# Layer 0's input loaded in a turned layout, and its ternary weights made later, in a two-layer transformer kernel on one core

## What is computed

```python
x = _layernorm(x + _L0_attn_ref(x, w_qkv, w_out, b_out))
    # qkv = x @ w_qkv; 16 heads of 16; causal softmax(q k^T / 4) v; @ w_out + b_out
x = _layernorm(x + _L0_ffn_ref(x, W_up, W_gate, W_down))
    # scale = mean(|W|) + 1e-8; W -> clip(round(W / scale), -1, 1) * scale
    # (silu(x @ wu.T) * (x @ wg.T)) @ wd.T
x = _layernorm(x + _L1_attn_ref(x, ...))      # windowed, global and with linear biases
x = _layernorm(x + _L1_ffn_ref(x, ...))
```

## Time and profile before

| | |
|---|---|
| median of 3 runs | 1007.37 us (1007.07 to 1007.87) |
| time of the profiled execution | 1006.18 us |
| its span | 1004.5 us, 18031 instructions |
| PE busy | 950.5 us (95%) |
| PE weight loads | 516.3 us (51%) |
| DVE busy | 690.4 us (69%) |
| ACT busy | 593.1 us (59%) |
| POOL busy | 354.1 us (35%) |

### The profile page before, as it was taken

The page is one execution under the profiler, slowest core; times in us unless marked ns, Lnnn a source line. Parts: engine busy times, 40 slices in busy tenths (PEclk is TensorE's granted clock), DMA queues, the critical chain, the costliest instruction groups (busy, mean ns, idle before and its releaser), DMA issues. The chain is left out here.

```text
span 1004.5 us, 18031 instructions
## 1 busy us (share of the span) xinstructions
PE 950.5 (95%) x6546; PEld 516.3 (51%) x6546; DVE 690.4 (69%) x1529; ACT 593.1 (59%) x1210; POOL 354.1 (35%) x424
## 2 busy tenths in 40 slices
PE   6798999999998999988899999999999998999997
PEld 4453333333344887664334344343434354798896
DVE  2778888888843687578888888888888632433423
ACT  3434777777766345436577777777777767222321
POOL 3022123321222455234446354352615333323432
PEclk9798999999999999999799999999999999999999
DMA  7644111222000200152705142130401000000001
GB/s 245 198 157 123 48 39 43 65 64 64 2 2 15 81 1 8 45 176 55 221 2 177 29 150 84 53 118 19 136 1 40 2 1 1 1 1 22 22 1 42
DMA packets 32996, 64.20 MB, mean 64 GB/s; under 512 B 6095, under 2 KB 22367, under 8 KB 30532
## 3 DMA queue, kind: packets, MB, share of 16 engines
q1 hardware_dynamic: 31564, 58.47, 18.9%
q0 software_dynamic: 1072, 3.80, 1.1%
q10 hardware_dynamic: 272, 0.79, 0.2%
HBM read 50.45 MB, written 12.32 MB: 62 GB/s over the span
## 5 line engine op out<-in xcount | busy, mean ns | idle before, releaser
L1150 ACT ACTIVATE prob<-ps 128x512 f32<-128x512 f32 (+6 forms) x896 | 426.9, 541 | 158.9 <-PE ps L1195 155.9
L1195 PE MATMUL ps<-qop,kop 98*128 98x512 bf16 (+14 forms) x1376 | 271.4, 288 | 1.7 <-ACT prob L1150 0.6
L1181 PE MATMUL ps<-kop,qop 96*128 96x512 bf16 (+3 forms) x896 | 245.2, 359 | 14.8 <-DVE maxes L1080 11.2
L1195 PEld LDWEIGHTS ps<-qop,kop 107*128 107x128 bf16 (+1 forms) x1376 | 113.3, 97 | 212.8 <-ACT prob L1150 118.8
L1224 PE MATMUL ps<-prob,vst 128*32 128x512 f32 (+4 forms) x1792 | 211.2, 543 | 4.7 <-POOL prob L1017 2.9
L1080 DVE CUSTOM_DVE_ANT_0 sums<-ps,tri 128x128 bf16<-128x128 f32 (+7 forms) x256 | 180.6, 754 | 20.5 <-PE ps L1181 18.9
L1017 POOL TENSOR_TENSOR prob<-prob,keep 128x384 int32<-128x384 int32 (+2 forms) x144 | 121.7, 854 | 190.4 <-ACT prob L1150 189.9
L1080 DVE CUSTOM_DVE_ANT_0 sums<-ps,table 128x960 bf16<-128x960 f32 x128 | 148.0, 1156 | 48.2 <-PE ps L1181 35.9
L1625 PE MATMUL ps<-xs,wffn 128*128 128x512 f32 x640 | 156.1, 396 | 1.0 <-PEq L829 1.0
L1080 DVE CUSTOM_DVE_ANT_0 tri<-ps,table 128x960 bf16<-128x960 f32 x128 | 147.6, 1153 | 3.0 <-PE ps L1181 2.9
L1520 POOL TENSOR_TENSOR hs<-hf,hs 128x512 fp32r<-128x512 f32 x64 | 83.0, 1297 | 150.6 <-ACT hs L1543 142.3
(11 more groups left out here) (106 smaller groups left out, 693.0 us busy)
## 6 DMA issues: line engine op xcount, KB each, us to landing
table<-in_table SPq DMA_DIRECT2D x32, 464.0 KB, 4.5
qop<-q_parts SPq DMA_DIRECT2D x96, 128.0 KB, 2.6
kop<-k_parts SPq DMA_DIRECT2D x48, 128.0 KB, 2.6
kop<-k_parts SPq DMA_DIRECT2D x48, 96.0 KB
q_parts<-qop SPq DMA_DIRECT2D x8, 384.0 KB, 3.8
q_parts<-kop SPq DMA_DIRECT2D x8, 384.0 KB, 2.6
x<-in_x SPq DMA_DIRECT2D x4, 512.0 KB, 6.1
k_parts<-qop SPq DMA_DIRECT2D x4, 384.0 KB, 2.7
```

The lines of the kernel that those rows point to most:

```text
L1150: nc.scalar.activation(prob[0:rows, q % 2, k % HG, lo % CH:lo % CH + hi - lo], ps[0:rows, home["exp", n, k], lo % CH:lo % CH + hi - lo], A ...
L1181: last = nc.tensor.matmul(ps[:, S_BANK + score_slot(L, k)[0] + a // CH, a % CH:a % CH + b - a], qop[0:RD, par, h, i0:i0 + P], kop[0:RD, pa ...
L1195: return nc.tensor.matmul(ps[:, bank, a % CH:a % CH + b - a], lhs, rhs, start=start, stop=True, skip_group_check=True)
```

## The change

1. The host also hands over x transposed (`xt`, 256 x 2048). Four transfers of 512 KB bring it straight into `proj.xt`: the first two as SP's first work, the other two behind the constants. Layer 0 has no turns any more. `K.x` is loaded behind group 2's operands, in four transfers, for the residual steps of groups 1 to 4, and `ident` is first waited for by the transposition of group 0's output.
2. The opening's order: units 0 to 3 come first, then v and units 4 to 7, then v 2, 3 and 4; one v of batch 1 (the last) is put behind the last maximum. Four banks of PSUM take turns instead of three. The steps beside the maxima are spread by the maxima's columns plus 256. Load 1 of the operands comes behind the writes of units 8 to 11.
3. POOL asks for the weight matrices only once group 0's operands have landed. The abs steps lie behind units 10, 11 and 12; total and threshold behind group 0's rows.
4. The ternary step is cut in 12 slices of 128x512. POOL makes the lower comparison into a bf16 buffer `below` of its own, four slices in quads 4 to 7 of each of groups 0, 5 and 6. DVE makes the second comparison, three slices in each of the last four quads of group 6. The feed-forward waits for all 12 slices.

```diff
+BELOW_GROUPS, BELOW_QUADS = (0, N - 3, N - 2), (4, 5, 6, 7)
@@ plan_by_table
+        if group in BELOW_GROUPS and n in BELOW_QUADS:
+            steps.append(("below", 4 * BELOW_GROUPS.index(group) + BELOW_QUADS.index(n), 0))
+        if group == N - 2 and n >= nq - 4:
+            steps += [("ternary", 3 * (n - nq + 4) + k, 0) for k in range(3)]
@@ opening_of
-PE_SHARE = ({"turn": 1, "unit": 1, "v": 1}, {"turn": 0.85, "unit": 1.72, "v": 1.72})
+PE_SHARE = ({"turn": 0.6, "unit": 1, "v": 1}, {"turn": 0.85, "unit": 1.72, "v": 1.72})
...
+    width = [hi - lo if layer.index == 1 else hi - lo + 2 * P for _, _, lo, hi in units]
...
+    scale = [("total", 0, 0), ("threshold", 0, 0)] if layer.index == 0 else []
+    return out + [("parts", 0, 1), ("rows", 0, 1)] + scale + [("max", k, 2) for k in range(AHEAD[layer.index])]
@@ Projection
-        banks = ((4, 5, 6), (4, 5, 6)) if i == 0 else ((6, 7), (6, 7, 4, 5))
+        banks = ((4, 5, 6, 7), (4, 5, 6, 7)) if i == 0 else ((6, 7), (6, 7, 4, 5))
...
+        if self.i == 0 and b == 0:
+            return [u[0], u[1], f[0], u[2], f[1], u[3], f[2], f[3], v[0], u[4], u[5], f[4], v[1], u[6], f[5], u[7], f[6],
+                    v[2], f[7], v[3], ("v", TB // 2)]
         if self.i == 0:
...
+            return [u[0], u[1], f[0], u[2], f[1], ("abs", 0), u[3], f[2], ("abs", 1), v[1], u[4], f[3], ("abs", 2),
+                    u[5], f[4], v[2], u[6], f[5], u[7], f[6], f[7], v[3]]
@@ pool
+        elif what == "below":
+
+            j, cols, home = self.slice_of(k)
+            pool.wait_ge(self.tern, 3)
+            nc.gpsimd.tensor_scalar(self.below[:, home], self.raw[j][:, cols], self.thr[:, 1, j:j + 1], None, ALU.is_lt
+                                    ).then_inc(self.below_set, 1)
@@ dve
         elif what == "ternary":
-            dve.wait_ge(self.tern, 3 + 2 * k)
-            nc.vector.tensor_scalar(self.below, self.raw[k], self.thr[:, 1, k:k + 1], None, ALU.is_lt
-                                    ).then_inc(self.tern, 1)
...
+            j, cols, home = self.slice_of(k)
+            dve.wait_ge(self.tern, 3)
+            dve.wait_ge(self.below_set, k + 1)
+            nc.vector.scalar_tensor_tensor(out=K.wffn[:, j, 0, cols], in0=self.raw[j][:, cols],
+                                           scalar=self.thr[:, 0, j:j + 1], in1=self.below[:, home],
+                                           op0=ALU.is_gt, op1=ALU.subtract).then_inc(self.tern, 1)
@@ sync
+                for c in range(NC // 2):
+                    load_turned(c)
                 sp.dma_start(K.ident[:], dram.ident).then_inc(proj.ident_loaded, 16)
...
+                for c in range(NC // 2, NC):
+                    load_turned(c)
...
-            later = len(proj.units) // 2 + 2 * (1 - i)
+            later = len(proj.units) // 2 + 4 * (1 - i)
...
             operands.load(sp, BUFS - 1)
+            if i == 0:
+                for c in range(NC):
+                    sp.dma_start(K.x[:, CT * c:CT * c + CT, :],
...
@@ gpsimd
             pool.wait_ge(fills, FILLS)
+            if i == 0:
+                pool.wait_ge(loaded[0], 16 * operands.loads)
+                for j, wt in enumerate(dram.ffn[0]):
...
```

113 lines of the change are left out of this document (55 added, 58 removed).

## The result

| | before | change |
|---|---|---|
| median | 1007.62 us (1007.07 to 1008.41, 4 runs) | 1000.39 us (999.68 to 1003.08, 4 runs) |
| profiled execution, its span | 1006.18, 1004.5 us | 1003.08, 1001.3 us |

The ratio is 0.9933, 95% interval 0.9912 to 0.9953: faster, by 7 us instead of the 17 of the prediction, and outside its range of 983.0 to 995.5. Measured again beside other kernels it was 999.18 us (998.53 to 1003.58, 6 runs), ratio 0.9940 (0.9917 to 0.9964).

What follows compares the result with a forecast made beforehand. Up to 86 us a chain (x, units 0 to 3, write, load, 32 maxima, rows) sets the pace, then PE is full. First exponential gains 17.7 us; less 0.3 and 0.4, 17.0: 989.5 us, range 983.0 to 995.5.

Steps and rivals of the forecast that it cites:

- step 3: Opening: ACT's first sum waits for late weights, holding DVE and PE; 3.0 us plus 1.0 for PE's clock, bounds 0 to 8.
- step 2: Group 0's stretch of maxima, without four turns and one v: 30.5 us, between engines' own work and upper bound 33.1.
- step 1: Start: x lands at 6.9, no turns ahead, DVE's first maximum at 30.3 instead of 46.19; 15.9 us gained, bounds 12 to 17.
- Step 4: Total and threshold behind group 0's rows, partly on the path of group 1's maxima: cost 0.3 us, 0 to 0.8.
- Step 5: Ternary slices ahead of group 7's first gathering: 12 take 7.5 us, with POOL's comparisons mostly in idle time; cost 0.4, 0 to 3.
- two engines block each other: Rival near group 7's gathering: DVE slices and POOL's clearings hold each other up; 3 us more, 992.5; chance 0.10.
- Step 6: Loading K.x behind group 2's operands and load 1 behind unit 11's write: both in time, no cost.
- The rival of a slow comparison on POOL: POOL's ternary comparisons delay quad 8's clearing and PE in three groups; at 5.5 us each, 1019 us; chance 0.03.
- the first exponential (68.6): Sign that the opening's gain arrived: group 0's first exponential at 68.6 us against 86.32, a gain of 17.7.
- the stretch took over 39 us: Sign of being wrong: group 0's stretch of maxima takes over 39 us.
- more than 2 us of the gain at the first exponential: Sign of being wrong: over 2 us of the lead at group 0's first exponential are missing at the kernel's end.
- group 7's gathering at about 286: Mark for the gathering behind the ternary slices, which ran at 278.70 before: it would run at about 286 us.

Runs made afterwards that it cites:

- constants ahead: The change plus 22 unused matmuls of ones on PE while it waits for its first operands: 1001.37 us, ratio 0.9945.
- own matrices: The change, with each sum of magnitudes waiting only for its own weight matrix instead of all three: 994.55 us, measured again 995.69 us.
- the small clearings: The sums late, with GpSimd's causal clearing cut to 8 elements in group 7 (992.64 us), then groups 6 and 7 (992.21 us) of layer 0.
- the sums late: The change, with three sums of magnitudes moved behind unit 13's finish, v 6 and unit 14's finish: 992.79 us, measured again 995.80 us.

## Why the prediction was wrong

The direction and the places were right, the size was not: the forecast gain was 17.0 us, the median's is 7.2, and the profiled execution's 3.1. What failed are three terms of the sum, all ahead of the first exponential: step 3 (3.8 us too small), step 2 (3.2) and step 1 (2.4). The gain there was 7.8 us (78.51 against 86.32) and not 17.7. The largest, step 3, failed because the first sum of magnitudes waits for all three matrices, and not for the one it reads. Against the change's profile, by the steps:

**Step 1, the start: 15.9 us forecast, 13.5 measured.** "x is SP's first transfer, 0.45 us earlier, so it lands at about 6.9" took the landing of x for the start. The unit needs w too. Before, it landed at 5.7 (4.9 us after its request at 0.80), and PE was at its turns until 10.78; now it lands 7.3 us after its request, and PE waits until 8.10. Why it lands later stays open. It isn't the bytes asked for alone: with as many as before the change it took 7.1 us, and with 0.5 MB less 6.8. What the traces show beside it is that the queue of x had moved 1199 packets (1.13 MB) by 8 us before, and 596 packets (1.07 MB) in the change, so packets twice as large, beside the same 272 packets of w. No run tested it. And "two units take 3.85 us at first" was read behind 3.4 us of turns, that is from a PE already at work: the first units now come from rest, 1.9 us slower in sixteen records than with constants ahead. Before, PE came from rest at the turns, which took 3.4 us for sixteen records (eight take 1.09 us at full clock). The writes took 3.0 us to land against 2.6. From the loads' request to the first score it was 9.6 us, as said (9.8).

**Step 2, the stretch without the weights: 30.5 us forecast, 33.7 measured** (33.1 was my upper bound). Of the eleven profiles in which nothing waited for the weights six had 33.6 to 33.7 us and five 34.9 to 35.2. What parts them is one piece of PE's work at a lower clock: the v above, or the first unit of batch 1, which took 2.95 to 3.36 us in the other four, at a granted clock of 0.57 to 0.65, where it takes 1.94. In these four PE had waited 2.0 to 3.9 us for the keys before the first score. I chose near the sum of busy times. DVE had its 27 us of work, 27.13 of the 33.6 with own matrices, but waits for ACT's first parts six times, 6.1 us together: a unit passes PE, ACT and DVE in turn, and DVE, in order, stands until its turn comes. My error was to stay near the sum of busy times where three engines hand work to each other. That these waits are what lies between 30.5 and 33.7 is read from the trace; no run took them away.

**Step 3, the weights: 4.0 us forecast, 7.8 measured** (41.5 less 33.7; 5.8 in the second profile). The mechanism and its order were right. The request came 3 us later than forecast (32.78 for 29.7), since it hangs on group 0's operands, and the last matrix landed at 48.1 and not at 41 to 44. The wait was 5.98 us where 3.0 were charged, and PE's clock behind it cost 1.5 where 1.0 was: 3.5 of the 3.8. The code of the wait was in the diff's surroundings and I read it as "the weights"; that the first sum needs a third of what it waits for would have made this step zero, as the kernel with own matrices did.

**Step 4, the scale: 0.3 us,** and from the first exponential to group 7 the lead falls from 7.8 to 7.6.

**Step 5, the slices: 0.4 us forecast, 1.2 measured in all eleven profiles with the change's slices, and 1.6 more in four of them.** Without clearings beside them twelve slices take 8.0 us (forecast 7.5). The rest, 9.70 in all, is the rival "two engines block each other", to which I gave 0.10: it was true, an overlap adding up to 0.38 us to a slice. I priced it at 3 us; of the 1.2 us that the slices cost, 0.5 went with the small clearings, and of the rest no run shows the cause. The room of 0.7 us at the gathering was real, and used up twice over.

**Step 6: nothing, as said.** The rival of a slow comparison on POOL is out: 1.56 us each, four in 6.2 us of 12, and the clearing behind them still finds POOL idle for 6 us or more. The two rows that I took for it, 0.64 and 1.15 us, were both too low, and it didn't matter.

Of my marks, the first unit (6.9), the last maximum (65) and the first exponential (68.6) were missed. Two of the signs that I had named as what would make me wrong came: the stretch took over 39 us, and in the first profile more than 2 us of the gain at the first exponential, 7.8 us, were missing at the end, where it was 3.2. In the second profile it was 8.7 and 7.7, so that this sign is of some executions only. The mark "group 7's gathering at about 286" forgot to take off the gain: by my own sum it is 269, and the gathering ran at 280.70.

The 1.5 us between the feed-forward and layer 1's parts, 155.8 us before and 157.3 in the change, came and went between profiles of the same kernel (155.8 in the change's second). Over all kernels it was 155.8 to 158.4, with the granted clock in 430 to 460 us between 0.83 and 0.94. What decides it was not tested. From group 0's last maximum to group 7's it took 194.3 to 198.1 us. These two, and PE's first records, are why gains under 2 us could not be shown by medians here.

## What to carry to other kernels

When a step is moved to where its input is late, look at what its wait counts: one semaphore for three transfers makes the first user wait for the last. Work that is removed at the start may have been hiding two other things, a landing and an engine's slow first instructions; ask what is there first when it is gone. And where a chain hands work from engine to engine, take the time of a stretch from the old one less what is removed, not from the busiest engine's sum.

The best versions here are the change with the sums late (992.8 and 995.8 us) and the change with a semaphore for each matrix (994.6 and 995.7): 11 to 15 us under the kernel before, each against the runs beside it, and 3.4 and 4.6 under the change where it was measured beside them (999.18 us).

## What was not expected of the hardware

- The profile gives the granted clock as 1.00 while the first matmuls after rest take 1.06 us instead of 0.59. The clock row does not show this; the duration of one instruction does.
- Beside back-to-back DVE slices with two SBUF inputs, of 0.74 us each, an 8-element GpSimd clearing took 1.24 us instead of 0.19, longer than one slice.
- A pause of 0.65 us at the gathering was followed by half clock in the change's first profile and by full clock in its second, at the same place of the same program; over all kernels with this pause it was half clock in four of eleven profiles.
